# Routed blocks: TensorE reads the expert numbers of the blocks three at a time, at ten chosen steps, instead of one in front of each block

## The reference, cut to what matters

```
probs = softmax(xf @ gate_w.T)                # 2048 tokens, 8 experts
topw, topi = top_k(probs, 2)                  # two experts for each token, weights normed to 1
routed = sum over experts e of  (silu(xf @ gate[e].T) * (xf @ up[e].T)) @ down[e].T * comb[:, e]
x = x + shared_ffn(xf) + routed               # hidden width 352
```

## Time and profile before

| what | value |
|---|---|
| runs | 845.48, 848.89, 854.44 us |
| median | 848.89 us |
| span of the profiled execution, first to last instruction | 877.9 us |
| time of the profiled execution beyond that span | not given for this kernel |
| TensorE busy | 779.2 us, 89% |
| VectorE, ScalarE, GpSimd busy | 614.2, 505.4, 411.7 us |
| mean granted TensorE clock | 0.963 of full speed |
| the routed blocks | 365 to 519 us of the span |

### The profile page before, as it was taken

One profiled execution on the slowest core, in us unless ns is written; L12 is line 12 of the kernel. 1 busy time (PEld: TensorE's weight loads), 2 busy tenths in 40 slices (PEclk: granted clock), 3 DMA queues, 4 the chain that ended last, 5 costly groups with the idle time before them and its releaser, 6 DMA issues.

```text
span 877.9 us, 13857 instructions
## 1 busy us (share of the span) xinstructions
PE 779.2 (89%) x4602; PEld 459.7 (52%) x4602; DVE 614.2 (70%) x1611; ACT 505.4 (58%) x863; POOL 411.7 (47%) x466
## 2 busy tenths in 40 slices
PE   5889999999999988875968998789999999999986
PEld 2454344444454433665948876445555555554544
DVE  6877778687787889661314758778778787787555
ACT  3336666666656665333614646356767777776672
POOL 3506775766665764443060177884572231311121
PEclk9879999999999999997987999999999999999999
DMA  9300000000000000311221102000000000000001
GB/s 352 146 0 1 2 1 0 1 1 1 1 1 1 1 0 22 91 51 46 70 63 34 46 26 96 13 25 1 1 1 1 1 1 1 1 1 1 1 1 49
DMA packets 14539, 25.35 MB, mean 29 GB/s; under 512 B 3174, under 2 KB 9192, under 8 KB 14344
## 3 DMA queue, kind: packets, MB, share of 16 engines
q1 hardware_dynamic: 11798, 18.85, 6.3%
q0 software_dynamic: 2048, 4.20, 1.6%
q10 hardware_dynamic: 626, 1.43, 0.5%
HBM read 15.03 MB, written 9.44 MB: 28 GB/s over the span
## 4 chain that ended last, share of the span: by engine, by line
PE 33%; DVE 15%; POOL 6%; issue 4%; another core or an unknown queue 3%; ACT 2%; DMA 0%; ACTq 0%; POOLq 0%; DVEq 0%
PE ps L1666 6%; PE ps L1751 6%; PE ps L1731 4%; DVE ps L2524 3%; PE ps L1637 3%; DVE mx_part L2527 3%; PE ps L1619 2%; PE ps L1629 2%; PE ps L1621 2%; PE ps L1620 1%; POOL xnT L658 1%; PE ps L1584 1%; PE ps L1759 1%; PE ps L1820 1%
## 5 line engine op out<-in xcount | busy, mean ns | idle before, releaser
L2042 DVE TENSOR_REDUCE mx_part<-ps 128x1 f32<-128x512 f32 x256 | 163.6, 682 | 59.5 <-PE ps L1312 58.8
L1109 ACT ACTIVATE pt<-ps 128x1024 f32<-128x1024 f32 (+1 forms) x160 | 149.7, 938 | 75.3 <-PE ps L1731 70.4
L906 ACT ACTIVATE pt<-ps 128x512 f32<-128x512 f32 x256 | 140.9, 596 | 69.6 <-PE ps L1337 63.2
L1666 PE MATMUL ps<-rounded 128*128 128x128 f32 (+2 forms) x352 | 124.8, 387 | 15.8 <-DVE mx_part L2524 7.7
L2524 DVE CUSTOM_DVE_ANT_0 ps<-ps,wm 128x128 f32<-128x128 f32 (+3 forms) x256 | 120.0, 519 | 18.9 <-PE ps L1666 16.9
L1337 PE MATMUL ps<-rounded 100*128 100x512 f32 x256 | 120.9, 484 | 10.9 <-ACT pt L906 9.7
L858 ACT ACTIVATE rounded<-ps 128x512 fp32r<-128x512 f32 (+3 forms) x160 | 94.4, 592 | 55.9 <-PE ps L1301 20.1
L721 POOL TENSOR_SCALAR_AFFINE_SELECT pt<-pt 128x512 f32<-128x512 f32 x64 | 40.1, 638 | 168.8 <-ACT pt L1109 168.7
L1731 PE MATMUL ps<-rounded 128*128 128x512 f32 (+2 forms) x352 | 116.4, 371 | 0.7 <-ACT rounded L858 0.7
L1312 PE MATMUL ps<-rounded 98*128 98x512 f32 x256 | 104.1, 429 | 3.4 <-DVE mx_part L2042 2.7
L2527 DVE TENSOR_REDUCE mx_part<-ps 128x1 f32<-128x512 f32 x128 | 82.3, 686 | 28.6 <-PE ps L1666 28.5
(11 more groups left out here) (307 smaller groups left out, 1305.6 us busy)
## 6 DMA issues: line engine op xcount, KB each, us to landing
wm<-in_wm SPq DMA_DIRECT2D x1, 4896.0 KB, 15.9
to_experts<-kstage SPq DMA_DIRECT2D x6, 512.0 KB, 4.6
of_experts<-pt SPq DMA_DIRECT2D x12, 256.0 KB, 2.0
kstage<-to_experts SPq DMA_DIRECT2D x10, 256.0 KB, 2.7
wm<-in_experts SPq DMA_DIRECT2D x1, 1540.0 KB, 7.5
x<-in_x SPq DMA_DIRECT2D x4, 256.0 KB, 5.9
out<-x SPq DMA_DIRECT2D x4, 256.0 KB, 2.3
early<-in_wo ACTq DMA_DIRECT2D x1, 512.0 KB
```

The source lines that it names most:

```text
L906: nc.scalar.activation(pt0(k, i), ps[:, ST0_BANKS[i % 2], :], ACT.Exp, scale=SCALE0).then_inc(exp_done, 1)
L1109: nc.scalar.activation(pt[:, 4 * (t % 2) + 2 * g:4 * (t % 2) + 2 * g + 2, 0:w], ps[:, ST1_BANKS[2 * g]:ST1_BANKS[2 * g] + 2, 0:w], ACT.Exp ...
L1666: ins = mm(bank[:, o:o + w], queries1(u, i), keys[:, 0:w], start=(o == 0), stop=(o == parts[-1][1]))
L2042: v.tensor_reduce(mx_part[u % 2][:, o:o + 1], ps[:, max_bank(u, n), :], AX_X, ALU.max).then_inc(max_done, 1)
```

## The change

The reads leave `block_up`. A table says before which step which numbers are read: blocks 0 to 2 before the loop, then three more at each of the steps 0 to 4 (up to block 17), three at each of the steps 17 to 21 (up to block 32), and from step 32 on one in each step, for the block that this step starts, as before. The wait for the second half's numbers moves from step 22 to step 17. Steps 5 to 16 and 22 to 31 read nothing. There are 46 reads before and after.

```diff
+EXPERT_LOADS = {-1: range(0, 3), **{i: range(3 * i + 3, 3 * i + 6) for i in range(5)}, 17: range(18, 21), 18: range(21, 24),
+                **{i: range(24 + 3 * (i - 19), 27 + 3 * (i - 19)) for i in range(19, 22)}, **{i: (i + 1,) for i in range(32, N_ALL - 1)}}
+LATER_LOADS = 17
...
+            def block_expert_ids(i):
+                for n in EXPERT_LOADS.get(i, ()):
+                    expert_of[n] = pe.value_load(block_i[0:1, n // NB, n % NB:n % NB + 1], min_val=0, max_val=E0 - 1)
+
             def block_up(n):
                 q, k = QUAD_OF[n], PLACE[n]
-                e = expert_of[n] = pe.value_load(block_i[0:1, n // NB, n % NB:n % NB + 1], min_val=0, max_val=E0 - 1)
+                e = expert_of[n]
...
             pe.wait_ge(block_ok, 1)
+            block_expert_ids(-1)
             block_up(0)
             for i in range(N_ALL):
                 c = SHARED_AT.get(i)
+                if i == LATER_LOADS:
+                    pe.wait_ge(block_ok, B)
+                block_expert_ids(i)
                 if c is None:
                     block_up(i + 1)
...
                     shared_down(2)
-                    pe.wait_ge(block_ok, B)
                     block_up(NB)
```

More of the change, by code:

```diff
@@ L196 @@
 SHARED_AT = {NB - 1: 2, N_ALL - 1: 3}
+EXPERT_LOADS = {-1: range(0, 3), **{i: range(3 * i + 3, 3 * i + 6) for i in range(5)}, 17: range(18, 21), 18: range(21, 24),
+                **{i: range(24 + 3 * (i - 19), 27 + 3 * (i - 19)) for i in range(19, 22)}, **{i: (i + 1,) for i in range(32, N_ALL - 1)}}
+LATER_LOADS = 17
+assert [n for i in sorted(EXPERT_LOADS) for n in EXPERT_LOADS[i]] == list(range(N_ALL))
 SECOND_FRONT = {2: (14, 3), 3: (37, 2)}
```

## The result

The changed kernel takes 861.37 us (median of four runs, 855.22 to 867.70) against 850.04 us for the kernel before (four runs, 845.48 to 854.44): ratio 1.0133, interval 1.0083 to 1.0183. It is slower by 11 us. The forecast was 856 us, in a range of 830 to 865. The ratios here are estimates over the runs with a 95% interval, and need not equal the quotient of the two medians.

What follows compares the result with a forecast made beforehand. TensorE's chain of waits was taken as the bound, with 33.1 us of pauses mostly the recording's. 844.8 us without pauses, +11.7 for batches, -0.4 for removed reads gave 856 us, range 830 to 865.

Steps and rivals of the forecast that it cites:

- Placement: Reads leave both GpSimd stretches: early ones some 4 us before the second scatter, later ones clear of the first gathers.
- A batch's price: Three reads at 0.65 us each idle TensorE 1.30 us before a step; ten batches, less cover, cost 11.7 us.
- Reads removed: 22 steps lose their read; as reads are hidden today, this gains 0.4 us at most.
- Sum: +11.7 for the batches and -0.4 for removed reads: +11.3 us of TensorE, moving the kernel's end by the full sum.
- The base: Traced span 877.9 less 33.1 of pauses: 844.8 us, 4.1 below the median, taken as the time without pauses.
- the pauses: TensorE's half-idle stretches, 387 to 407 and 449.5 to 469 us, beside GpSimd's second scatter and first gathers: 33.1 us.
- The remote waits: Waits with unknown releaser before the silu, multiply and copies; if gone, the reads cause the pauses. 44.6 us over two lines.
- a shorter trace with a longer median: A trace 22 us shorter with a longer timed median would confirm that the pauses are mostly the recording's.
- Rival 1: Timed runs pause too, at GpSimd's stretches, and reads cause it: all 33.1 us go, 827 us; chance 0.27 with its middle.
- Rival 2: TensorE's dense signals or the recording cause the pauses; they stay and the reads cost: 860 us; chance 0.13.
- Rival 3: TensorE's clock falls to half speed on the batches' new gaps: +9 us, so 865; chance 0.09.
- Rival 4: Grouped reads overlap, so the batches cost about 2 us: 847 us, no change; chance 0.13.

Runs made afterwards that it cites:

- e2: The kernel before with only the batches of three at steps 0 to 4, then one read a step from step 17: 852.20 us, ratio 1.0030.
- e6: The kernel before with the expert number read once, before block 0, and used for all 46 blocks (another routed result): 879.12 us, ratio 0.9948.
- e1: The kernel before, unchanged, run and recorded once more: 850.47 us, ratio 1.0004.
- e10: The kernel before with experts fixed at build time, no reads and no register offsets (another routed result): 846.23 us, ratio 0.9938.
- the halves: Two kernels, each the kernel before with half of the batches: steps 0 to 4 only, ratio 1.0030; steps 17 to 21 only, ratio 1.0049.
- e5: The changed kernel, unchanged, measured a second time in another job: 895.91 us against 881.87 for the kernel before, ratio 1.0152.
- e4: The changed kernel with one load instruction for a batch's numbers in one half, bounds unchecked: 848.93 us, ratio 0.9992 to the kernel before.
- e12: The kernel before with the second scatter as SyncE's plain DMAs and fixed experts for blocks 23 to 45 (another routed result): 864.43 us, ratio 0.9804.
- e11: The kernel before with GpSimd's second scatter replaced by sixteen plain DMAs of SyncE (another routed result): 851.94 us, ratio 1.0020.

## Why the prediction came out as it did

*Placement.* Right: the early reads end at 393 us, some 3 us ahead of the second scatter, whose last issue starts at 415.2; those for blocks 18 to 32 lie between 420.5 and 435, and the next one comes at 466.8, after the first gathers' last issue at 463.2. The scatter came later with the counts, as said, and nothing waited for it.

*A batch's price.* The mechanism and the unit were right: 0.65 us a read, one behind the other. The gaps before blocks 18 to 22 are 0.65 to 1.17 us, where 1.2 to 1.3 was said. Where the forecast gave 6.04 us for the later five (5 x 1.30 - 0.46), the trace has 5.79 (16.15 against 10.36). The early five were mis-sized: 5.64 forecast, 3.72 measured from block 0 to 5 (16.27 against 12.55), and 0.31 of it given back by block 8. The gaps before blocks 1 to 5 are 0.59, 0.16, none, 1.72 and none. The forecast priced these steps at full speed. TensorE was granted half speed from 378 to 385 us, around blocks 0 to 2, so the work in its queue lasted longer and covered most of three batches. Behind the idle time of 1.72 us it was granted half speed once more, for 3.4 us, and this covered the fifth batch but made step 4 itself 3.17 us long instead of 1.99 (the first two lines are of the first trace of the changed kernel, the third of e2):

```profile
391.40:394.90 3.50, 3.50 (x16) 3.31 (x15) 2.48 (x11) 1.19 (x3) 0.00 (x0) 0.51 0.00 0
...
390.57 0.43 PE L1627 MATMUL ps<-rounded,qstage 128*128 x1 [1.72 <-issue]
...
382.20:385.60 3.40, 3.30 (x15) 3.00 (x14) 2.85 (x13) 0.97 (x4) 0.00 (x0) 0.50 0.00 0
```

*Reads removed.* Forecast -0.4 us as most of it, with "hidden today" as the reason. Measured -1.7: 18.68 us against 19.48 from block 8 to 17, and 67.33 against 68.24 from 22 to 45. e6 shows why: the reads of the kernel before cost 4.6 us in all, where I had taken them to be free but for 0.04 us a step. Steps that begin the front of layer 1 lay more of a read open (from block 34 to 35 it is 4.16 us in e1, 3.60 in e10).

*Sum.* 11.3 us forecast for TensorE, 7.5 in the traces (3.72 - 0.31 - 0.80 + 5.79 - 0.91). The timed 11.3 us has the interval 7 to 16, the second measurement 11 to 16, and the halves give 6.7. The equality of 11.3 and 11.3 is chance: the timed difference holds some 4 us more than the blocks do, which no term of the sum has and which go at least in part with the clock in front of the blocks (e5).

*The base.* This step failed. The forecast took the span without the pauses, 844.8 us, as what a timed run would keep, and so gave the change 4.1 us that it did not have. The runs showed in its place: timed runs of the low level hold no pause at all, and the kernel before without pauses is 847.4 us of span and 1.8 around it, 849.2, the timed median. The spread of the runs that I read as pauses of some size goes with the clock: of the runs of before beside e1, those at a mean granted clock of 0.984 took 847 to 849 us, those at 0.962 took 860. What I had right is that the timed runs had no room for the pauses. What I had wrong is why: not the recording, since the timed runs of the high-level jobs are 32 us longer as well. Two of the signs that the prediction set misled for the same reason. The remote waits were gone from the changed kernel's trace, which was to mean that the reads are the cause; they are gone from e1's too, with the reads in place. And a shorter trace with a longer median was to mean that the pauses are the recording's; it meant that the two traces were of different levels.

*The rivals.* Rival 1 (the reads cause the pauses) is refuted by e5 and e6. Rival 2 is what happened in its first part, another cause, and in its arithmetic, the cost on top of an unchanged rest. But the pauses could not stay in the timed runs of the result, which never had them, and of its two causes the recording is out; the other, TensorE's dense signals, was not tested. Its 860 us is the nearest number, and its argument, the read of ordinary length in the middle of a pause, was the best evidence in the trace. Rival 3 (the clock falls on the gaps) did not come for the five later batches, which ran at clock 1.00. For the early ones it came in small: half speed for 3.4 us behind the gap of 1.72 us, in all three traces that have these batches of checked reads (the two of the change and e2), while the six other traces of the low level have none there. The changed kernel's trace is 18.6 us longer than e1's, 7.5 of it in the blocks; block 0 starts 7.2 us later, before anything that the change touches, in a stretch granted 0.97 of the clock where e1 has 1.00:

```profile
60.00:340.00 280.00, 267.43 (x1446) 124.31 (x1445) 214.54 (x346) 176.56 (x334) 178.63 (x145) 0.97 0.00 1
```

Rival 4 (grouped reads overlap) is refuted for three instructions, and holds in another form: one instruction that loads three registers takes 0.76 us. The Trainium skill ("DMA: Bandwidth & Descriptors", section "Latency and other measured facts") has a floor of about 600 ns for the load of a register, which unrolling amortizes. Here the load itself takes 0.30 us, half of that; the 0.65 us that the prediction set beside the floor are the load with its bounds check. Where several registers go into one instruction, e4 agrees that the cost of each falls; where separate loads only stand together, the trace of the change speaks against it.

## What to carry to other kernels

A sequencer's reads hide only under the work that already lies in its engine's queue: one in each step was nearly free here (4.6 us for 45), a second cost 0.47 us and a third about 0.7, so gathering hidden reads into batches lays them open unless one instruction loads them all. A stall that lines up with a piece of code in one trace need not be made by it; record the same program again in another job before you build on it. And where the traced span is far above the timed runs, that gap is itself the finding: the trace shows something that the timed runs do not have.

## What the runs showed that was not expected

The same program has two levels, 850 and 882 us, from job to job, and the difference sits in two stretches of the trace where GpSimd issues indirect DMAs beside the routed blocks. The engines that wait for TensorE there go on up to 14 us late, when TensorE itself has long gone on: in the trace of before, the multiply of block 8 starts at 401.96, and the last gate or up matmul of block 9 had started 5.65 us before it. Where on the way the signal is held up, no trace shows.

```profile
396.31 0.32 PE L1621 MATMUL ps<-rounded,x_lo 128*128 x1
```

Writing the second scatter's bytes by plain DMAs of SyncE instead took its 18 us away (e12) and cost nothing measurable where there was no pause (1.0020, interval 0.9984 to 1.0057, in e11). It is no remedy as it stands, since the rows then lie unsorted.

One load of three registers takes 0.76 us, of one 0.30 us; three checked reads, each a load and its bounds check, take 1.95 us.
